# A decoder layer with routed experts: expert rows turned by VectorE, a shorter router, products of the identity in front

## The chip, the cores and the metric

One core of one Trainium2 chip runs the whole layer as one program. The metric is the device time of one execution in microseconds (us). The engines are TensorE (PE; its weight loads are PEld), VectorE (DVE), ScalarE (ACT), GpSimd (POOL) and the queue that issues the transfers, SyncE (SP). Each runs its own instructions in order; semaphores tie them together.

## The reference, cut to what matters

The layer is self-attention, cross-attention and a mixture of experts, each followed by a residual sum and a layer norm, on 8 x 112 = 896 rows of 512 numbers, in float32.

```
x = layernorm(x + attention(x))                 # 16 heads of 32, banded mask
x = layernorm(x + cross_attention(x, context))  # 16 heads of 128, 375 context rows, q and k normalised
scores = sigmoid(x @ gate_w.T)                  # 8 experts
topk   = top_k(scores + gate_bias, 2)           # two experts for each row
w      = scores[topk] / sum(scores[topk])
out    = silu(g) * y @ shared_dw.T              # shared part, hidden width 704
for e in experts: out += (silu(g_e) * u_e) @ down_w[e].T * w_e   # hidden width 352
x = layernorm(x + out)
```

## The kernel before, in words

Nearly every product of two float32 matrices is made of three one-pass products of a high and a low part (`three_products`, lines 86 to 88): ACT rounds a block to its high part, DVE or POOL subtracts to get the low part, PE multiplies. A few small or less exact ones are plain float32 products, which the profile records twice for each product.

**Start.** SP loads two blocks of weights, then the turned input `xT` in four pieces, one for each 128 rows of features, then `wv`. ACT makes `xT_hi` half a piece at a time, DVE `xT_lo`. PE waits for the first `xT_lo` and begins the 48 products of the first projections. The identity `ident` and the mask are set by POOL; a semaphore `consts_set` counts to 8 when both are there.

**Cross-attention.** Slots of one pair of heads and one batch element each, in a hardware loop. Its last slots are written out by hand, so that the last output products (`output(t, bank)`, t = 2 to 6), the residual sums, the layer norm and the turning of the result (`turn(pe, t)`) run into each other. In that order stand `output(4, y_ps)`, then a wait for the sum that reads `y_ps` (`added(4)`), then `join` (the last 12 value products, into the same bank, `o_view`), `turn` 2 and 3, `output` 5 and 6, `turn` 4, the first shared up-product `dense_up(0)`, `turn` 5 and 6, and then the router.

**Router.** `logits_T` makes the eight logits of all rows (24 products of 448 columns), ACT copies them, `logits` turns them back in seven small products, ACT takes the exponential, DVE chooses two experts for each row (`choose`, result `picked`). `places` counts on PE, with `before` (a strict triangle of ones) and `every` (all ones), how many earlier rows chose the same expert: one product, six that carry the earlier tiles on, and seven that make the total. DVE makes from it the owner of each block and the slot of each row (`place`). POOL then scatters the 896 rows twice to `sorted_x` in DRAM, SP fetches weights by owner.

**Shared part and blocks.** The shared hidden width is done in two units of 352, A ahead of the blocks and B behind them: `dense_up(k)`, then `dense_down(unit, t)` for t = 0 to 6. Between them lie NB = 21 blocks of 128 sorted rows. For block j, PE does:

```
block_up(j)        # 24 products of 352 columns: 4 pieces of x by 2 halves by 3
turn_block(j + 1)  # 4 float32 transposes of the next block's rows into PSUM
block_down(j - 1)  # 3 plain float32 products of 512 columns
turn_hidden(j)     # 3 transposes of the hidden rows
```

`turn_block(0)` stands ahead of `dense_down(0, 6)`. ACT does for each block: silu, `block_x(j + 1)` (the high part of the turned rows, read from PSUM), the copy of the turned hidden rows, and `up_high(j + 2)`, four casts that round the up-weights of the block after next. DVE does: two of the four low parts of these weights (`up_low`), the product of the hidden halves, `block_low(j + 1)` (the low part of the rows, one input in PSUM, one in SBUF), and the copy of an output block (`take`). POOL does the other two low parts.

SP's order for block j is: `load_up(j + 4)` once `block_up(j)` is done, `load_x(j + 3)`, `load_down(j + 3)`, `store_y(j - 1)`. The weights have a ring of three buffers. A block moves 1408 KB of up-weights, 768 KB of down-weights, 256 KB of rows in and 256 KB out. After the last block, unit B's `dense_up` needs the up-weights of load 22 (`LAST_U`), which go the same way as a block's.

## Time and profile before

| | |
|---|---|
| median of three runs | 1074.83 us (1074.69 to 1076.5) |
| the profiled execution | 1065.3 us |
| its span, first to last instruction | 1063.6 us |
| PE / PEld / DVE / ACT / POOL busy | 96% / 85% / 66% / 49% / 50% |
| granted TensorE clock, mean | 0.999 |
| share of PE in the chain that ended last | 74% |

The profiled execution is 1.7 us longer than its span, and 9.5 us shorter than the median of the three runs. The cross-attention loop ends at about 785 us, the router lies between 812 and 830 us, the blocks between 860 and 1010 us, unit B behind them.

### The profile page before, as it was taken

What the parts mean: (1) busy time and instruction counts of PE and PEld (TensorE: products, weight loads), DVE (VectorE), ACT (ScalarE), POOL (GpSimd) and SP (SyncE); (2) the same over time, 40 slices, a digit from 0 to 9 for tenths busy, and PEclk for the clock granted to TensorE, in tenths of its full rate; (3) what the DMA queues carried; (4) which work ended last, traced back from release to release, by engine and by line L of the source; (5) the groups of instructions that cost most, each with busy time, mean ns of one, the idle gap of its engine ahead of it and who ended that gap; (6) DMA issues with size and microseconds to landing.
All of it is one profiled execution on the core that took longest, in us unless ns stands there. A gap on an engine that the chain in (4) does not pass through costs nothing.

```text
span 1063.6 us, 20152 instructions
## 1 busy us (share of the span) xinstructions
PE 1021.0 (96%) x7006; PEld 906.5 (85%) x7006; DVE 703.5 (66%) x1452; ACT 523.7 (49%) x1033; POOL 530.0 (50%) x515
## 2 busy tenths in 40 slices
PE   6999888999999999999999999999998999999997
PEld 5866667899999999999999999999886887887786
DVE  4277776777777777777777777767785454554457
ACT  5355545555545555555555455455542345655520
POOL 0156766864633633643643643643572645444543
PEclk9999999999999999999999999999999999999999
DMA  8100104324333233233233233224220769999843
GB/s 285 69 31 2 60 16 136 149 113 147 121 112 116 95 110 115 95 110 115 94 110 115 96 108 115 98 107 152 91 73 1 299 243 376 389 390 378 309 120 108
DMA packets 44697, 153.46 MB, mean 144 GB/s; under 512 B 3704, under 2 KB 3704, under 8 KB 41568
## 3 DMA queue, kind: packets, MB, share of 16 engines
q1 hardware_dynamic: 42400, 145.38, 38.0%
q0 software_dynamic: 2240, 7.34, 2.1%
q8 instruction: 34, 0.56, 0.2%
q14 instruction: 23, 0.19, 0.0%
HBM read 130.04 MB, written 22.66 MB: 144 GB/s over the span
## 4 chain that ended last, share of the span: by engine, by line
PE 74%; DVE 4%; POOL 3%; issue 2%; ACT 2%; POOLq 0%; DVEq 0%; ACTq 0%
PE xa_y_ps L86 6%; PE xa_y_ps L88 6%; PE xa_y_ps L87 5%; PE ex_raw_ey_ps L2078 5%; PE ex_raw_gu_ps L86 4%; PE ex_raw_gu_ps L88 4%; PE ex_raw_gu_ps L87 4%; PE xa_c_ps L1871 4%; PE xa_c_ps L1867 4%; PE xa_c_ps L1866 4%; PE xa_turn_ps L1948 3%; PE xa_turn_ps L1904 3%; PE front_k_ps L86 3%; PE front_k_ps L88 3%; PE front_k_ps L87 3%
## 5 line engine op out<-in xcount | busy, mean ns | idle before, releaser
L1218 POOL TENSOR_TENSOR xa_probs<-xa_probs,xa_inv_sum 112x750 f32<-112x750 f32 x63 | 97.8, 1552 | 75.8 <-DVE xa_inv_sum L1545 75.8
L1494 DVE TENSOR_TENSOR xa_kT_lo<-xa_turn_ps,xa_kT_hi 128x750 fp32r<-128x750 f32 x63 | 59.2, 940 | 99.8 <-ACT xa_kT_hi L1306 99.7
L1203 POOL TENSOR_TENSOR k_ms<-k_ss,sum_eps 125x6 f32<-125x6 f32 x63 | 12.5, 198 | 210.9 <-DVE k_ss L1510 210.9
L1866 PE MATMUL xa_c_ps<-xa_probsT_hi,xa_nat 125*128 125x224 f32 x384 | 92.3, 274 | 2.7 <-ACT xa_probsT_hi L1322 2.7
L1867 PE MATMUL xa_c_ps<-xa_probsT_hi,xa_nat 125*128 125x224 f32 x384 | 92.3, 275 | 0.0
L1206 POOL TENSOR_TENSOR k_inv<-k_ms,neg_half 125x6 f32<-125x6 f32 x63 | 83.4, 1324 | 8.3 <-POOL k_ms L1203 6.6
L1322 ACT CAST xa_probsT_hi<-xa_turn_ps 125x672 fp32r<-125x672 f32 x62 | 44.6, 719 | 87.1 <-PE xa_turn_ps L1948 87.1
L1328 ACT ACTIVATE xa_probs<-xa_scores_ps,xa_bias,xa_q_scale 112x375 f32<-112x375 f32 x126 | 82.6, 662 | 5.7 <-DVE xa_bias L1520 4.4
L1866 PEld LDWEIGHTS xa_c_ps<-xa_probsT_hi,xa_nat 125*128 125x128 f32 x384 | 73.6, 192 | 3.5 <-issue 3.1
L1867 PEld LDWEIGHTS xa_c_ps<-xa_probsT_hi,xa_nat 125*128 125x128 f32 x384 | 73.5, 191 | 0.5
L86 PE MATMUL front_k_ps<-land_xa_wk_hi,land_xa_ctx 128*125 128x256 f32 x252 | 71.4, 283 | 1.4 <-DVE front_k_hat L1537 1.0
L87 PE MATMUL front_k_ps<-land_xa_wk_hi,land_xa_ctx 128*125 128x256 f32 x252 | 70.9, 281 | 0.0
L88 PE MATMUL front_k_ps<-land_xa_wk_lo,land_xa_ctx 128*125 128x256 f32 x252 | 70.8, 281 | 0.0
L1302 ACT ACTIVATE front_k_sq<-front_k_ps 125x512 f32<-125x512 f32 x63 | 37.7, 598 | 61.5 <-PE front_k_ps L88 60.2
L1871 PE MATMUL xa_c_ps<-xa_probsT_lo,xa_nat 125*128 125x224 f32 x384 | 64.0, 275 | 0.7 <-DVE xa_probsT_lo L1526 0.7
L1510 DVE TENSOR_REDUCE k_ss<-front_k_sq 125x6 f32<-125x768 f32 x63 | 59.7, 948 | 5.6 <-ACT front_k_sq L1310 5.6
L416 POOL TENSOR_TENSOR sa_masked<-sa_masked,sa_row_max 112x448 f32<-112x448 f32 x32 | 30.2, 945 | 66.1 <-DVE sa_row_max L647 65.4
L1489 DVE TENSOR_TENSOR xa_cT_lo<-xa_c_ps,xa_cT_hi 128x448 fp32r<-128x448 f32 x61 | 38.0, 623 | 37.9 <-ACT xa_cT_hi L1297 37.9
L1310 ACT ACTIVATE front_k_sq<-xa_k_ps 125x256 f32<-125x256 f32 x63 | 24.2, 385 | 70.8 <-PE xa_k_ps L88 70.8
L1516 DVE TENSOR_REDUCE xa_row_max<-xa_scores_ps 112x2 f32<-112x750 f32 x63 | 58.5, 928 | 0.0
L1297 ACT CAST xa_cT_hi<-xa_c_ps 128x448 fp32r<-128x448 f32 x61 | 32.5, 533 | 52.7 <-PE xa_c_ps L1871 52.7
L1526 DVE TENSOR_TENSOR xa_probsT_lo<-xa_turn_ps,xa_probsT_hi 125x672 fp32r<-125x672 f32 x62 | 53.1, 857 | 5.3 <-ACT xa_probsT_hi L1322 4.7
(371 smaller groups left out, 3486.4 us busy)
## 6 DMA issues: line engine op xcount, KB each, us to landing
xa_nat<-ctx_split SPq DMA_DIRECT2D x56, 750.0 KB
ex_raw_raw<-in_w_units SPq DMA_DIRECT2D x15, 1408.0 KB, 7.7
ex_raw_raw<-in_w_units SPq DMA_DIRECT2D x15, 768.0 KB, 7.7
land_ex_raw<-in_w_units SPq DMA_DIRECT2D x8, 1408.0 KB, 7.7
land_ex_raw<-in_w_units SPq DMA_DIRECT2D x8, 768.0 KB, 7.7
ctx_split<-xa_nat SPq DMA_DIRECT2D x8, 750.0 KB
sorted_x<-ex_raw_y_sb SPq DMA_DIRECT2D x7, 768.0 KB, 10.5
ex_raw_x_nat<-sorted_x SPq DMA_DIRECT2D x21, 256.0 KB, 8.1
```

The lines of the kernel that those rows point to most:

```text
L86: pe.matmul(out, st_hi, mv_hi, start=first, stop=False)
L87: pe.matmul(out, st_lo, mv_hi, start=False, stop=False)
L88: return pe.matmul(out, st_hi, mv_lo, start=False, stop=last)
L1206: pool.tensor_tensor(k_inv[0:KT, :], k_ms[0:KT, :], env["neg_half"][0:KT, 0:2 * KT_N], ALU.pow).then_inc(sem["kinv_done"], 1)
L1218: pool.tensor_tensor(probs[0:T, u % 2], probs[0:T, u % 2], inv_sum[0:T, u % 2, :].unsqueeze(2).broadcast_to([T, 2, KV]), ALU.mult).then_in ...
L1328: act.activation(probs[0:T, u % 2, h, :], scores_ps[0:T, h, 0:KV], ACT.Exp, bias=bias[0:T, u % 2, h:h + 1], scale=q_scale[0:T, u % B // HA ...
L1494: dve.tensor_tensor(kT_lo[:, :, 0:KV], turn_ps[:, :, 0:KV], kT_hi[:, :, 0:KV].bitcast(F32), ALU.subtract).then_inc(sem["kT_lo_done"], 1)
L1510: dve.tensor_reduce(k_ss[0:KT, :], k_sq[0:KT, :].rearrange("p (a d) -> p a d", d=XA_DH), AX_X, ALU.add).then_inc(sem["kss_done"], 1)
L1516: dve.tensor_reduce(row_max[0:T, u % 2, :], scores_ps[0:T, :, 0:KV], AX_X, ALU.max).then_inc(sem["max_done"], 1)
L1866: pe.matmul(c_view[:, c], nat[0:KT, u % 2, 0, at], probsT_hi[0:KT, :, cols], start=(t == 0), stop=False)
L1867: pe.matmul(c_view[:, c], nat[0:KT, u % 2, 1, at], probsT_hi[0:KT, :, cols], start=False, stop=False)
L1871: mm = pe.matmul(c_view[:, c], nat[0:KT, u % 2, 0, at], probsT_lo[0:KT, :, cols], start=False, stop=(t == KT_N - 1))
```

## The change

It has eight parts.

1. The input `xT` is loaded in eight pieces instead of four, each with a semaphore of its own, and ACT waits for each half.
2. PE waits for `consts_set` 8 and makes sixteen float32 products of the identity with itself before it waits for the first weights.
3. The last `join` writes to a bank of `turn_ps` (`o_last`) and stands ahead of the wait `added(4)`, which moves behind `turn` 2 and 3.
4. `turn` 5 and 6 stand inside `dense_up(0)`, behind 18 of its 24 products.
5. The gate's high and low part lie side by side (`gate_hl`), so that one product makes both: 16 products instead of 24. The seven turns are 16 wide, begin when the first half is copied, and DVE adds the two parts (`logits_added`) ahead of the exponential.
6. `before`, `every` and `picked` become one-pass operands; the seven products of the total become one, and DVE sums its result.
7. `turn_block` leaves PE. The rows of a block are fetched by four transfers, each into 32 partitions in runs of 128 numbers (512 bytes), and DVE turns them in squares of 32 into `x_raw` in SBUF, in one instruction; `block_x` and `block_low` read `x_raw`. The experts' up-weights are reordered on the host to suit. `turn_block(j + 1)` stands first in DVE's work for block j.
8. `turn_block(0)` and `block_low(0)` follow DVE's sum of tile 5, and `dense_down(0, 6)` moves behind `block_up(0)`.

```diff
             for c in range(DC):
-                sp.dma_start(xT_raw[:, c, :], xT[:, c, :]).then_inc(sem[f"xT_{c}_loaded"], 16)
+                for g in range(2):
+                    cols = slice(g * HT, (g + 1) * HT)
+                    sp.dma_start(xT_raw[:, c, cols], xT[:, c, cols]).then_inc(sem[f"xT_{c}_{g}_loaded"], 16)
...
+            wait(pe, "consts_set", 8)
+            for _ in range(16):
+                pe.matmul(y_ps[:, 0:P], ident[:], ident[:], start=True, stop=True)
             wait(pe, "wq_lo_done", 1)
...
+        o_last = turn_ps[:, 0, 0:4 * T].rearrange("p (h t) -> p h t", h=2)
...
             def load_x(j):
                 if j >= 2:
                     sp.wait_ge(xs["xb_turned"], j - 1)
-                sp.dma_start(x_nat[:, j % 2, :], sorted_x[j * P:(j + 1) * P, :]).then_inc(xs[f"x_{j % 2}_loaded"], 16)
+                rows = sorted_x[j * P:(j + 1) * P, :].rearrange("(b t) d -> t b d", t=SQUARE)
+                for a in range(P // SQUARE):
+                    part = x_nat[a * SQUARE:(a + 1) * SQUARE, j % 2, :].rearrange("t (b d) -> t b d", d=P)
+                    sp.dma_start(part, rows[:, :, a * P:(a + 1) * P]).then_inc(xs[f"x_{j % 2}_loaded"], 16)
...
-                act.copy(xb_hi[:], et_ps[:, 0, :]).then_inc(xs["xb_hi_done"], 1)
+                act.copy(xb_hi[:], x_raw[:]).then_inc(xs["xb_hi_done"], 1)
...
+            def turn_block(j):
+                dve.wait_ge(xs[f"x_{j % 2}_loaded"], 64 * (j // 2 + 1))
+                if j >= 1:
+                    dve.wait_ge(xs["xb_lo_done"], j)
+                dve.transpose(x_raw[:].rearrange("p (c b t) -> p b c t", c=DC, t=SQUARE), x_nat[:, j % 2, :].rearrange(
+                    "p (b c t) -> p b c t", c=DC, t=SQUARE)).then_inc(xs["xb_turned"], 1)
...
-                dve.tensor_tensor(xb_lo[:], et_ps[:, 0, :], xb_hi[:].bitcast(F32), ALU.subtract).then_inc(xs["xb_lo_done"], 1)
+                dve.tensor_tensor(xb_lo[:], x_raw[:], xb_hi[:].bitcast(F32), ALU.subtract).then_inc(xs["xb_lo_done"], 1)
...
+                dve.wait_ge(xs["logits_ready"], 1)
+                pair = et_ps[:, 0, 0:2 * TILES * E].rearrange("p (t a e) -> p t e a", a=2, e=E)
+                dve.tensor_reduce(score[:], pair, AX_X, ALU.add).then_inc(xs["logits_added"], 1)
                 dve.wait_ge(xs["logits_exp"], 1)
...
-            block_low(0)
-            add_shared(TILES - 1, 0)
+                if t == TILES - 2:
+                    turn_block(0)
+                    block_low(0)
             for j in range(NB):
                 n = UPS + j
+                if j + 1 < NB:
+                    turn_block(j + 1)
                 up_low(j + 2)
...
-                        mm = three_products(pe, et_ps[0:E, g, 0:HT], gate_hi[:, c, :], gate_lo[:, c, :],
-                                            xT_hi[:, c, cols], xT_lo[:, c, cols], c == 0, c == DC - 1)
+                        pe.matmul(et_ps[0:2 * E, g, 0:HT], gate_hl[:, c].rearrange("p a e -> p (a e)"), xT_hi[:, c, cols],
+                                  start=(c == 0), stop=False)
+                        mm = pe.matmul(et_ps[0:E, g, 0:HT], gate_hi[:, c, :], xT_lo[:, c, cols], start=False, stop=(c == DC - 1))
...
-                for t in range(TILES):
-                    mm = pe.matmul(et_ps[:, 1, 0:E], every[:], picked[:, t, :], start=(t == 0), stop=(t == TILES - 1))
-                mm.then_inc(xs["places_ready"], 1)
-
-            def dense_up(k, base, w_hi, w_lo):
+                pe.matmul(et_ps[:, 1, 0:TILES * E], every[:], picked[:].rearrange("p t e -> p (t e)"), start=True,
+                          stop=True).then_inc(xs["places_ready"], 1)
+
+            def dense_up(k, base, w_hi, w_lo, between=None):
...
             output(4, y_ps)
-            added(4)
-            join(N + 2, 0, N // 2 - 1)
+            join(N, 0, N // 2 - 1, o_last)
             turn(pe, 2)
             turn(pe, 3)
+            added(4)
...
             for t in range(TILES - 1):
                 dense_down(0, t, 0)
-            turn_block(0)
-            dense_down(0, TILES - 1, 0)
             pe.wait_ge(xs["consts_set"], 2)
             for j in range(NB):
                 block_up(j)
-                if j + 1 < NB:
-                    turn_block(j + 1)
-                if j >= 1:
+                if j == 0:
+                    dense_down(0, TILES - 1, 0)
+                else:
                     block_down(j - 1)
                 turn_hidden(j)
```

## Rows read from the trace of the kernel before

**Rows 1.** The page: busy us (share) xinstructions of each engine.
```profile
PE 1021.0 (96%) x7006; PEld 906.5 (85%) x7006; DVE 703.5 (66%) x1452; ACT 523.7 (49%) x1033; POOL 530.0 (50%) x515
```

**Rows 2.** Timeline of the start: start us, duration us, engine, line, operation [idle before].
```profile
2.08 0.59 POOL L383 TENSOR_SCALAR_AFFINE_SELECT sa_mask<-sa_mask 112x448 f32<-112x448 f32 x1
9.06 0.71 PE L86 MATMUL sa_scores_ps<-xT_hi,sa_qk_hi 128*128 128x448 f32 x1 [9.06 <-DVE xT_lo L580]
12.94 0.37 PE L87 MATMUL sa_scores_ps<-xT_hi,sa_qk_lo 128*128 128x448 f32 x1
20.54 0.39 PE L86 MATMUL sa_proj_ps<-land_wv_wv_hi,xT_hi 128*112 128x512 f32 x1
```

**Rows 3.** Timeline, the end of cross-attention and the router, 797 to 823 us.
```profile
798.48 0.34 PE L86 MATMUL xa_y_ps<-xa_cT_hi,xa_wv_hi 128*128 128x224 f32 x1 [0.87 <-DVE resid L1718]
798.40 2.09 POOL L112 TENSOR_SCALAR resid<-resid,ln_mv,ln_rstd 128x512 f32<-128x512 f32 x1
812.17 0.37 PE L86 MATMUL ex_raw_et_ps<-xT_hi,ex_raw_gate_hi 128*8 128x448 f32 x1 [1.56 <-DVE xT_lo L138]
817.85 0.60 PE L1988 MATMUL ex_raw_et_ps<-ident,ex_raw_logitsT 8*128 8x8 f32 x7 [0.61 <-ACT ex_raw_logitsT L1429]
```

**Rows 4.** Timeline, the counts of `places`.
```profile
823.48 1.46 PE L1998 MATMUL ex_raw_et_ps<-ex_raw_picked,ex_raw_every 128*128 128x48 f32 x12
824.80 1.71 PE L2001 MATMUL ex_raw_et_ps<-ex_raw_picked,ex_raw_every 128*128 128x8 f32 x14
```

**Rows 5.** Timeline, from unit A to the second block, 859 to 868 us.
```profile
859.17 0.60 PE L2042 MATMUL ex_raw_et_ps<-ident,ex_raw_x_nat 128*128 128x128 f32 x4
859.37 0.69 DVE L1674 TENSOR_TENSOR resid<-resid,ex_raw_ey_ps 128x512 f32<-128x512 f32 x1 [0.58 <-PE ex_raw_ey_ps L88]
861.70 0.33 PE L86 MATMUL ex_raw_gu_ps<-land_ex_up_lo,ex_raw_xb_hi 128*128 128x352 f32 x1
862.51 3.20 DVE L1572 TENSOR_TENSOR ex_low_low<-ex_raw_raw,land_ex_up_hi 128x704 fp32r<-128x704 f32 x2
862.51 4.74 POOL L1243 TENSOR_TENSOR ex_low_low<-ex_raw_raw,land_ex_up_hi 128x704 fp32r<-128x704 f32 x2 [9.18 <-ACT land_ex_up_hi L1354]
865.55 0.60 PE L2042 MATMUL ex_raw_et_ps<-ident,ex_raw_x_nat 128*128 128x128 f32 x4
```

**Rows 6.** Timeline of one steady block, from the end of `block_up` at 943.14 us.
```profile
943.14 0.60 PE L2042 MATMUL ex_raw_et_ps<-ident,ex_raw_x_nat 128*128 128x128 f32 x4
943.58 2.74 PE L2078 MATMUL ex_raw_ey_ps<-ex_raw_raw,ex_raw_hT 128*128 128x512 f32 x6
946.40 0.41 PE L86 MATMUL ex_raw_gu_ps<-land_ex_up_lo,ex_raw_xb_hi 128*128 128x352 f32 x1
949.28 3.48 POOL L1243 TENSOR_TENSOR ex_low_low<-ex_raw_raw,land_ex_up_hi 128x704 fp32r<-128x704 f32 x2 [3.68 <-ACT land_ex_up_hi L1354]
```

**Rows 7.** Windows: stretch, length; PE PEld DVE ACT POOL busy; PEclk, DMA share, GB/s.
```profile
871.50:878.67 7.17, 7.17 (x39) 5.66 (x38) 3.60 (x5) 4.22 (x7) 3.03 (x3) 1.00 1.02 397
878.67:1000.46 121.79, 121.79 (x631) 96.26 (x630) 61.19 (x85) 71.78 (x119) 59.26 (x35) 1.00 1.00 383
```

**Rows 8.** Transfers 242.6 to 243.9 us: packets by size; then the queue.
```profile
DMA packets 101, 0.16 MB, mean 119 GB/s; under 512 B 51, under 2 KB 51, under 8 KB 101
q1 hardware_dynamic: 101, 0.16, 34.0%
```

**Rows 9.** Up-weight transfers, 864 to 900 us, then 972 to 1000: KB, us to landing.
```profile
ex_raw_raw<-in_w_units SPq DMA_DIRECT2D x4, 1408.0 KB, 7.1
...
ex_raw_raw<-in_w_units SPq DMA_DIRECT2D x3, 1408.0 KB, 9.1
```

**Rows 10.** Timeline, last up-weight load, its casts, and unit B's first product.
```profile
993.48 0.34 SPq L1100 DMA_DIRECT2D ex_raw_raw<-in_w_units  x1
1004.37 2.83 ACT L1354 CAST land_ex_up_hi<-ex_raw_raw 128x704 fp32r<-128x704 f32 x4
1010.44 0.45 PE L86 MATMUL ex_raw_gu_ps<-xT_hi,land_ex_up_hi 128*128 128x448 f32 x1
```

More of the change, by code:

```diff
@@ L53 @@
 HPAD = HC * P
+SQUARE = 32
 def hold(eng, sem, i, per, n):
@@ L468, in _ @@
             for c in range(DC):
-                wait(act, f"xT_{c}_loaded", 16)
                 for g in range(2):
                     cols = slice(g * HT, (g + 1) * HT)
+                    wait(act, f"xT_{c}_{g}_loaded", 16)
                     act.copy(xT_hi[:, c, cols], xT_raw[:, c, cols]).then_inc(sem["xT_hi_done"], 1)
@@ L740, in _ @@
             values(0, range(DC))
-            wait(pe, "consts_set", 8)
             def scores(u):
@@ L1174, in set_consts @@
                           allow_small_or_imprecise_dtypes=True).then_inc(xs["more_consts"], 1)
-                pool.memset(before, 1.0).then_inc(xs["more_consts"], 1)
-                pool.memset(every, 1.0).then_inc(xs["more_consts"], 1)
+                pool.memset(before.bitcast(F32), 1.0).then_inc(xs["more_consts"], 1)
+                pool.memset(every.bitcast(F32), 1.0).then_inc(xs["more_consts"], 1)
                 pool.memset(upto, 1.0).then_inc(xs["more_consts"], 1)
                 pool.wait_ge(xs["more_consts"], 6)
-                pool.affine_select(out=before, in_=before, compare_op=ALU.is_gt, fill=0.0, base=0,
+                pool.affine_select(out=before, in_=before.bitcast(F32), compare_op=ALU.is_gt, fill=0.0, base=0,
                                    pattern=[[1, P]], channel_multiplier=-1).then_inc(xs["more_consts"], 1)
@@ L1618, in place @@
                 dve.wait_ge(xs["places_ready"], 1)
-                step(dve.tensor_tensor(over[:], et_ps[:, 1, 0:E].unsqueeze(2).broadcast_to([P, E, TILES]), level[:], ALU.is_gt))
+                step(dve.tensor_reduce(n_tiles[:], et_ps[:, 1, 0:TILES * E].rearrange("p (t e) -> p e t", e=E), AX_X, ALU.add))
+                step(dve.tensor_tensor(over[:], n_tiles[:].unsqueeze(2).broadcast_to([P, E, TILES]), level[:], ALU.is_gt))
                 step(dve.tensor_reduce(n_tiles[:], over[:], AX_X, ALU.add))
@@ L1873, in context_of, with join @@
                 mm.then_inc(sem["c_ready"], 1)
-            def join(s, i, j):
+            def join(s, i, j, view):
                 hold(pe, sem["wv_lo_done"], i, 1, j // HALF + 1)
@@ L1957, in slot @@
                 if j is not None:
-                    join(s, i, j)
+                    join(s, i, j, o_view)
                 u = s - 2
@@ L2016, in dense_up @@
                                             xT_hi[:, d, cols], xT_lo[:, d, cols], d == 0, d == DC - 1)
+                        if between is not None and (half, d) == (1, 1):
+                            between()
                 mm.then_inc(xs["up_ready"], 1)
@@ L2034, in dense_down @@
                 mm.then_inc(xs["y_ready"], 1)
-            def turn_block(j):
-                pe.wait_ge(xs[f"x_{j % 2}_loaded"], 16 * (j // 2 + 1))
-                if j >= 1:
-                    pe.wait_ge(xs["xb_lo_done"], j)
-                for c in range(DC):
-                    mm = pe.transpose(et_ps[:, 0, c * P:(c + 1) * P], x_nat[:, j % 2, c * P:(c + 1) * P], ident[:])
-                mm.then_inc(xs["xb_turned"], 1)
             def block_up(j):
@@ L2125, in _ @@
             added(2)
-            join(N, 0, N // 2 - 2)
+            join(N, 0, N // 2 - 2, o_view)
             context_of(u - 1, 0)
@@ L2148, in _, with last_turns @@
             pe.wait_ge(xs["up_lo_g"], 2)
-            dense_up(0, 0, up_hi, up_lo)
-            turn(pe, 5)
-            turn(pe, 6)
+            def last_turns():
+                turn(pe, 5)
+                turn(pe, 6)
+            dense_up(0, 0, up_hi, up_lo, last_turns)
             pe.wait_ge(norm["turn_lo"], TILES)
@@ L2240, with quarters, unit @@
     shared_gw, shared_dw = a["L0_ffn_shared_gw"], a["L0_ffn_shared_dw"]
-    def unit(up, down):
+    def quarters(w):
+        return w.reshape(P // SQUARE, DC, SQUARE, w.shape[1]).transpose(0, 2, 1, 3)
+    def unit(up, down, rows=chunks):
         tail = np.zeros((HC * P - HID, D), down.dtype)
-        return np.concatenate([chunks(up).reshape(P, -1), chunks(np.concatenate([down, tail], axis=0)).reshape(P, -1)], axis=1)
-    units = [unit(a["L0_ffn_up_w"][e].T, a["L0_ffn_down_w"][e].T) for e in range(EXPERTS)]
+        return np.concatenate([rows(up).reshape(P, -1), chunks(np.concatenate([down, tail], axis=0)).reshape(P, -1)], axis=1)
+    units = [unit(a["L0_ffn_up_w"][e].T, a["L0_ffn_down_w"][e].T, quarters) for e in range(EXPERTS)]
     for s in range(SHARED // HID):
```

53 lines of the change are left out of this document (30 added, 23 removed).

## Prediction

> **What bounds it now.** I read the page first: PE is busy 96% of the span [rows 1], so a gain is PE time removed, or a wait of PE removed. Then the timeline, at the four places that the change touches. At the start PE has nothing until 9.06 us, and then 48 products take until 20.54 us [rows 2]. Until 12.94 us they start 0.37 us apart, behind it 0.20. The clock column says full for both, but the ratio is that of 1.2 to 2.4 GHz, so I count 3.88 us at half speed. Near the router PE stands for 0.87, 1.56 and 0.61 us [rows 3]. From unit A to the second block it is nearly without gaps [rows 5], and in the blocks it has none: PE is busy 121.79 of 121.79 us over 17 blocks, 7.164 us each [rows 7]. The view that decides is the last column but one of the same row: the transfer engines are 1.00 busy as well, at 383 GB/s. A block moves 2688 KB, 2.75 MB, which at 383 GB/s is 7.2 us. So the blocks have two bounds at the same place. The landing times agree: an up-weight load lands 7.1 us behind its issue early on and 9.1 at the end [rows 9]. The queue grows slowly. What PE loses there, the transfers may not give back.
>
> **The start (parts 1 and 2).** The mask is set at 2.67 us [rows 2], so the sixteen products start at about 2.75. The trace shows no such product. Four transposes of 128 columns take 0.44 us [rows 6], 0.11 each and one record each; a plain float32 product is recorded twice, so I take 0.22 at full and 0.44 at half speed. With 3.9 us at half speed, as in [rows 2], nine products fill them, and the other seven end at 8.2 us. The first projection starts there instead of 9.06, since half a piece of input is there sooner: 0.85. All 48 then run at 0.20: 9.6 us instead of 11.48, 1.9. Together 2.7 us. If all sixteen ran at half speed they would end at 9.8, and 1.1 were left. Nothing behind is bound by time of day: PE is what later slots wait for, so I carry the gain through.
>
> **The router (parts 3 to 6).** The 0.87 us in front of the last `join` goes, but `turn` 3 still needs POOL, whose step that starts at 798.40 ends at 800.49 [rows 3]; I take 0.4 of it (0 to 0.87). With `turn` 5 and 6 six products of 0.2 earlier, their rounding lies beside these, and 1.25 of the 1.56 us goes. Eight gate products fewer are 1.6 us. The first three turns of the logits no longer wait: 0.2. In `places` 14 records take 1.56 us, from 824.80 to their last result, 0.11 each, and 12 take 1.3 [rows 4]. Small as they are, they cost their weight load, so one-pass products cost 0.11 each: eight instead of 27 records, 2.1 us less. DVE's two extra sums (about 0.25 each) lie beside `dense_up(1)`, and on the way to the slots, which still gets 1.8 shorter. Sum on PE: 0.4 + 1.25 + 1.6 + 0.2 + 2.1 = 5.55 us. Start and router give 8.25 (6.5 to 8.7).
>
> **From unit A to the blocks (part 8).** Before, `turn_block(0)` ran at 859.17, and `dense_down(0, 6)` covered the two rounding steps; `block_up(0)` started at 861.70 and ended at 865.55 [rows 5]. Now the cover is gone: DVE's sum of tile 5 ends at 860.06, then come DVE's turn, ACT's high part, DVE's low part. The turn is not in the trace; the nearest rows are 128x512 steps of DVE at 0.69 us, the upper bound twice that. I take 0.65 + 0.6 + 0.7 + 0.2 for hand-offs: start 862.2, end 866.05. PE stands 3 us. On this clock of before, the blocks start 0.5 us late.
>
> **The blocks (part 7).** PE drops four transposes, 0.44 us [rows 6]: 6.73 us a block. DVE (3.6 us a block) and ACT (4.2) have room [rows 7]. Two things do not shrink.
>
> First POOL: `block_up` at 946.40, POOL's two low parts from 949.28 to 952.76, needed at 953.56 [rows 6]: 6.36 us into the block, less than 6.73. But `block_low` now has both inputs in SBUF, as `up_low` has, and where two such DVE steps met POOL's they took 3.20 us, and POOL 4.74 instead of 3.48 [rows 5, 6]. One step of 0.69 would lengthen POOL by about 0.6: 7.06 us a block. The Trainium skill (SBUF — State Buffer, Who interferes with whom) says that DVE's second pair of ports is POOL's, and held exclusively for an instruction; rows 5 and 6 agree in kind.
>
> Second, the transfers. Their time for a block before lies between 6.93 (2.75 MB at the 397 GB/s of the best block shown) and 7.17 us [rows 7]; I take 7.1, because the queue grew. The rows' load changes from 128 packets of 2 KB to 512 of 512 bytes, 384 more. The price of a packet itself: in 1.3 us near 243 us, 34.0% of 16 engines is 7.07 us of engine time for 101 packets, 51 of them small, 0.16 MB [rows 8]. The bytes at 383 GB/s, 24 a nanosecond for one engine, take 6.7 of it, or 6.5 with the megabytes rounded down to 0.155; 0.4 to 0.6 us for 51 packets is 8 to 12 ns each. 384 such packets over 16 engines are 0.2 to 0.3 us. I take 0.43: the upper end and 0.13 more, because four transfers complete instead of one and may hinder each other (rival b). That makes 7.53 us a block (7.13 to 7.8). That is above PE's and POOL's.
>
> The sum on the clock of before: the first load of the series is issued at 866.4 and lands 7.2 later, 873.6; the 18th behind it, that of unit B, lands 18 x 7.53 = 135.5 later, at 1009.1. Three of ACT's four casts (2.12 of 2.83), POOL's 3.48 + 0.6 and 0.5 for hand-offs and for the rows' arrival ahead of DVE's low parts put unit B at 1015.8 instead of 1010.44 [rows 10]: 5.3 us lost. Before, issued at 993.48 and landed 9.1 later, the same load was there 1.8 us ahead of its cast at 1004.37. That was all the slack there was.
>
> **Total.** -8.25 + 5.3 = -2.95 us. Against the profiled execution's 1065.3 that is 1062.3; the median lies 9.5 above it, so 1071.9.
>
> **Rivals.** (a) The transfers have more to give than 383 GB/s. For it: the best block ran at 397. Against it: share 1.00 for 120 us, and the growing queue. Then POOL sets 7.06 us or PE 6.73. Unit B starts 20 x 6.73 + 2.8 behind 866.05, at 1003.4, 7.0 early, or with 7.06 at 1010.0: -8.7 in all with POOL (1066), -15.3 with PE (1059.5).
>
> (b) Slower: the narrow transfers. Each of the four fills 32 partitions. A load of 256 KB is 0.7 us of the 7.1; if its engines get in each other's way and it takes twice that, the block is 7.1 + 0.7 + 0.2 = 8.0 us, unit B 8.5 us later still than forecast, and the total +5.5 us (1080). It decides from 7.70 us a block, where the 8.25 are used up. Against it: the engines drift apart, and other transfers lie between. The Trainium skill (SBUF — State Buffer, Door 1: The DMA port swizzle) states it as a rule: partitions 0 to 31 reach 8 of 16 ports, half the rate, and two transfers in a row don't make up for it. No row here shows it; by its rate the load would take twice as long.
>
> (c) The front gives less: the 3 us that PE stands before `block_up(0)` cost it the clock as at the start, where 3.88 us at half speed cost 1.9. Then -1 us (1073.8). For it: no wait as long lies in the rows before a product at full speed, the longest is 1.56.
>
> **How the numbers follow.** The forecast 0.46 (1066 to 1075, by 7.2 to 7.7 us a block), (a) 0.16, (b) 0.24, (c) 0.14. 0.2% is 2.15 us, about what a measurement tells from no change, so faster ends at 1072.7: all of (a) and two thirds of the forecast, with a little of (c), 0.5. Same (to 1077.0), 0.26, from the rest of the forecast, (c), and the mild end of (b). Slower 0.24. Range 1064.5 to 1078.5: it leaves out PE-bound blocks below, and the narrow transfers at full price above.
>
> **What would show it.** PE starts projecting near 8.2 us with all starts 0.2 apart; seven turns of logits end 5 us earlier relative to 797 us; `places` takes under 1 us; about 3 us of idle PE ahead of `block_up(0)`; in the blocks PE waits, by name for the low parts of the up-weights, that is for a landing, at 7.5 us a block, with the share of the transfers at 1.00 and GB/s near 365. Blocks of 6.7 or 7.06 without waits for weights would be (a), of 8 us (b). Wrong would be, most of all, the price of a 512-byte packet: each 0.1 us a block is 1.8 us of the total.

## The result, and the profile after

The changed kernel takes 1082.38 us in the median of 11 runs (1080.44 to 1086.91), the kernel before in the same comparison 1075.86 us (11 runs, 1073.18 to 1079.27): ratio 1.0062, interval 1.0047 to 1.0078. It is slower by 6.5 us where I had forecast 2.95 us faster, and it lies above the range. The profiled execution took 1085.06 us, with a span of 1083.3.

First the page, busy time by engine; it answers to [rows 1]:

```profile
PE 1023.2 (94%) x6926; PEld 902.7 (83%) x6926; DVE 755.1 (70%) x1475; ACT 524.4 (48%) x1033; POOL 544.3 (50%) x515
```

TensorE has 80 records fewer and is a little longer busy, over a longer span. The timeline at the start, answering to [rows 2]:

```profile
2.72 6.28 PE L738 MATMUL sa_y_ps<-ident 128*128 128x128 f32 x32 [2.72 <-POOL sa_mask L387]
8.76 0.45 PE L87 MATMUL sa_scores_ps<-xT_hi,sa_qk_hi 128*128 128x448 f32 x1
9.04 0.36 PE L88 MATMUL sa_scores_ps<-xT_hi,sa_qk_lo 128*128 128x448 f32 x1
...
19.13 0.40 PE L87 MATMUL sa_proj_ps<-land_wv_wv_hi,xT_hi 128*112 128x512 f32 x1
```

The first projection starts 0.3 us earlier, and its products start 0.20 us apart nearly from the first on, TensorE's full speed. Near the router, answering to [rows 3, 4]:

```profile
798.50 0.66 PE L130 MATMUL xa_scores_ps<-ident,resid 128*128 128x128 f32 x4 [1.17 <-POOL resid L113]
...
808.45 0.38 PE L2009 MATMUL ex_raw_et_ps<-xT_hi,ex_raw_gate_hl 128*16 128x448 f32 x1 [0.35 <-DVE xT_lo L139]
...
812.49 0.42 PE L2020 MATMUL ex_raw_et_ps<-ident,ex_raw_logitsT 16*128 16x16 f32 x4 [0.33 <-ACT ex_raw_logitsT L1441]
...
817.79 0.19 PE L2028 MATMUL ex_raw_et_ps<-ex_raw_picked,ex_raw_before 128*128 128x56 f32 x1
817.81 0.81 PE L2031 MATMUL ex_raw_et_ps<-ex_raw_picked,ex_raw_every 128*128 128x48 f32 x6
818.48 0.27 PE L2033 MATMUL ex_raw_et_ps<-ex_raw_picked,ex_raw_every 128*128 128x56 f32 x1
```

All of that is as planned. From unit A to the blocks, answering to [rows 5]:

```profile
846.18 0.50 PE L87 MATMUL ex_raw_ey_ps<-land_ex_down_hi,ex_raw_h_hi 128*128 128x512 f32 x1 [3.79 <-DVE resid L1698]
...
848.18 0.63 PE L88 MATMUL ex_raw_ey_ps<-land_ex_down_hi,ex_raw_h_lo 96*128 96x512 f32 x1
...
856.96 0.70 DVE L1592 STREAM_TRANSPOSE ex_raw_x_raw<-ex_raw_x_nat 128x512 f32<-128x512 f32 x1
...
859.25 0.40 PE L87 MATMUL ex_raw_gu_ps<-land_ex_up_lo,ex_raw_xb_hi 128*128 128x352 f32 x1 [2.94 <-issue]
```

The 2.94 us in front of `block_up(0)` were in my sum. The 3.79 us were not. Five products later, from 847.75 us on, the down-products start 0.43 us apart instead of 0.23 for 3 us: TensorE's lower clock (1.2 GHz), granted 0.50 in that stretch. One block in the steady part, answering to [rows 6]:

```profile
942.50 0.40 PE L87 MATMUL ex_raw_gu_ps<-land_ex_up_hi,ex_raw_xb_hi 128*128 128x352 f32 x1 [1.15 <-DVE ex_raw_xb_lo L1600]
...
943.61 2.82 ACT L1366 CAST land_ex_up_lo<-ex_raw_raw 128x704 fp32r<-128x704 f32 x4 [1.74 <-DMA ex_raw_raw<-in_w_units]
...
944.98 0.71 DVE L1592 STREAM_TRANSPOSE ex_raw_x_raw<-ex_raw_x_nat 128x512 f32<-128x512 f32 x1 [1.98 <-DMA ex_raw_x_nat<-sorted_x]
...
945.62 3.14 DVE L1584 TENSOR_TENSOR ex_low_low<-ex_raw_raw,land_ex_up_lo 128x704 fp32r<-128x704 f32 x2
...
949.11 1.73 DVE L1600 TENSOR_TENSOR ex_raw_xb_lo<-ex_raw_x_raw,ex_raw_xb_hi 128x512 fp32r<-128x512 f32 x1
...
950.94 0.40 PE L87 MATMUL ex_raw_gu_ps<-land_ex_up_lo,ex_raw_xb_hi 128*128 128x352 f32 x1 [1.15 <-DVE ex_raw_xb_lo L1600]
```

From 942.50 to 950.94 is 8.44 us a block instead of 7.16. TensorE names VectorE as what it waits for, and the instruction is `block_low`, the low part of the rows; I had forecast a wait for the low parts of the weights. Two steps back on that chain both ScalarE's casts and VectorE's turn stand waiting for a transfer, one for weights, the other for rows. The windows and the transfers of the page, answering to [rows 7, 9]:

```profile
920.00:980.00 60.00, 51.35 (x240) 37.54 (x239) 45.95 (x44) 30.62 (x51) 31.29 (x15) 1.00 1.05 333
```

```profile
ex_raw_raw<-in_w_units SPq DMA_DIRECT2D x15, 1408.0 KB, 13.1
...
ex_raw_x_nat<-sorted_x SPq DMA_DIRECT2D x84, 64.0 KB, 10.6
```

The transfer engines are fully busy and move 333 GB/s, not 383. An up-weight load lands 13.1 us behind its issue in the median of the 15, not 7 to 9.

**The two profiles can't be compared as they stand.** They are 19.7 us apart, the medians 6.5. A second profile of the kernel before (`e0_before` below) has a span of 1073.6 instead of 1063.6, and both differences lie outside the blocks: 6.4 us up to the first block, in unit A, and 3.6 behind the blocks. The blocks took 7.16 us in both.

### The profile page after: what moved, and what is told of

It reads as the page before. It is cut to its first block, busy times and chain, and to the rows that moved or that the text cites. A ratio compares the mean times of both kernels' runs of the same rounds, so it can differ in the third digit from the quotient of the medians.

```text
span 1083.3 us, 20081 instructions
## 1 busy us (share of the span) xinstructions
PE 1023.2 (94%) x6926; PEld 902.7 (83%) x6926; DVE 755.1 (70%) x1475; ACT 524.4 (48%) x1033; POOL 544.3 (50%) x515
## 4 chain that ended last, share of the span: by engine, by line
PE 63%; DMA 6%; DVE 5%; issue 4%; POOL 4%; ACT 1%; SPq 1%; another core or an unknown queue 1%; POOLq 0%; DVEq 0%; ACTq 0%
PE xa_y_ps L87 6%; PE xa_y_ps L89 5%; PE xa_y_ps L88 5%; DMA ex_raw_x_nat<-sorted_x 5%; PE xa_c_ps L1900 4%; PE xa_c_ps L1896 3%; PE xa_c_ps L1895 3%; PE xa_turn_ps L1977 3%; PE xa_turn_ps L1933 3%; PE ex_raw_gu_ps L87 3%; PE ex_raw_gu_ps L89 3%; PE ex_raw_gu_ps L88 3%; PE front_k_ps L87 3%; PE front_k_ps L89 3%; PE front_k_ps L88 3%
## 5 line engine op out<-in xcount | busy, mean ns | idle before, releaser
L1538 DVE TENSOR_TENSOR xa_probsT_lo<-xa_turn_ps,xa_probsT_hi 125x672 fp32r<-125x672 f32 x62 | 53.1, 857 | 5.2 <-ACT xa_probsT_hi L1334 4.7
## 6 DMA issues: line engine op xcount, KB each, us to landing
ex_raw_raw<-in_w_units SPq DMA_DIRECT2D x15, 1408.0 KB, 13.1
land_ex_raw<-in_w_units SPq DMA_DIRECT2D x8, 768.0 KB, 13.1
```

## The experiments

The ratio is to the kernel before, run on the same chip. "Late blocks" is the mean distance of the starts of `block_up` over the last 13 blocks of the profile, from the timeline. e0 to e3 ran on one chip, e4 to e7 on a second, e8 to e12 on a third, e13 to e15 on a fourth; the kernel before took 1075.3, 1076.7, 1065.9 and 1066.0 us on them. "4 x 32, 512 B" is four transfers into 32 partitions each, in packets of 512 bytes; a load is called narrow when its transfers fill fewer than 128 partitions, and wide otherwise. The edits are shown shortened. e4 to e7 leave rows or features in the wrong places and so don't compute the layer; they do the same work and are there to measure only.

| run | rows' load | turned by | ratio (interval) | late blocks, us |
|---|---|---|---|---|
| kernel before (e0) | 1 x 128 partitions, 2 KB | PE | 0.9998 (0.9979 to 1.0017) | 7.16 |
| changed kernel | 4 x 32, 512 B | DVE | 1.0062 (1.0047 to 1.0078) | 8.49 |
| e1_front | 1 x 128, 2 KB | PE | 0.9926 (0.9900 to 0.9952) | 7.16 |
| e2_wide4 | 4 x 128, 512 B, dealt | DVE | 1.0298 (1.0271 to 1.0325) | 9.49 |
| e3_blocks (old front) | 4 x 32, 512 B | DVE | 1.0154 (1.0120 to 1.0188) | 8.22 |
| e4_narrow2k | 4 x 32, 2 KB | DVE | 1.0009 (0.9986 to 1.0032) | 8.02 |
| e5_wide2k | 1 x 128, 2 KB | DVE | 0.9889 (0.9855 to 0.9923) | 6.88 |
| e6_wide512 | 4 x 128, 512 B | DVE | 0.9890 (0.9856 to 0.9924) | 6.88 |
| e7_narrow_pe | 4 x 32, 512 B | PE | 1.0058 (1.0039 to 1.0076) | 8.41 |
| e8_order | 4 x 32, 512 B, order 0 2 1 3 | DVE | 1.0053 (1.0038 to 1.0068) | 8.09 |
| e10_act_queue | 4 x 32, 512 B, ScalarE's queue | DVE | 0.9974 (0.9959 to 0.9988) | 7.61 |
| e11_scatter | 1 x 128, 2 KB | PE | 0.9922 (0.9905 to 0.9939) | 7.16 |
| e12_halves | 2 x 64, 2 KB | PE | 1.0022 (1.0007 to 1.0037) | 8.13 |
| e13_three | as e10, three buffers | DVE | 0.9976 (0.9962 to 0.9990) | 7.52 |
| e14_start (parts 1, 2) | 1 x 128, 2 KB | PE | 0.9981 (0.9965 to 0.9996) | 7.16 |
| e15_front_again | 1 x 128, 2 KB | PE | 0.9925 (0.9909 to 0.9941) | 7.16 |

**e0_before**: the kernel before, unchanged.

> The kernel before, unchanged, for a second profile of it. The profile on record took 1065.3 us where its other executions took 1073 to 1079, and the changed kernel's profile took 1085.1 where its median is 1082.4: the two profiles are 19.7 us apart, the medians 6.5. If the executions differ in one place, this profile shows it: I expect the difference behind 785 us, either in the scatter of the rows (end of unit A), or in blocks that take 7.3 to 7.6 us instead of 7.16 because their transfers are slower. If the blocks take 7.16 here too and the time is near 1075, the difference lies elsewhere. Ratio 1.00.

Ratio 0.9998. The extra time is behind 785 us and not in the blocks. In unit A, TensorE's timeline and then ScalarE's:

```profile
855.85 0.79 PE L86 MATMUL ex_raw_ey_ps<-land_ex_down_hi,ex_raw_h_hi 128*128 128x512 f32 x1 [5.98 <-DVE resid L1674]
```

```profile
851.11 0.54 ACT L1369 ACTIVATE ex_raw_silu_g<-ex_raw_gu_ps 96x448 f32<-96x448 f32 x1 [8.44 <-remote]
```

The sum of tile 0 stands in VectorE's order behind the work on ScalarE's last silu, and that silu is late. It starts when the weights' and the scatter's transfers drain (their share falls from 0.95 to 0.21 at 851.0 us). In the first profile the transfers drained as late, and the same silu ran at 846.03; so why it waits here is open. The last part is longer too: from unit B's first product to the end 56.8 us instead of 53.1. It goes with the chip and not with the change: e0 to e7 show 55 to 58 us there, e8 to e15, on chips where the kernel before takes 1066 us, 53.1. (Each chip had one group of runs, so chip and hour can't be told apart.)

**e1_front** takes back parts 7 and 8:

```diff
-                for a in range(P // SQUARE):
-                    ...                                        # the four narrow transfers
+                sp.dma_start(x_nat[:, j % 2, :], sorted_x[j * P:(j + 1) * P, :]).then_inc(...)
-            dve.transpose(x_raw...)                            # block_x, block_low read x_raw
+            for c in range(DC): pe.transpose(et_ps[:, 0, ...]) # block_x, block_low read et_ps
```

> The change without parts 7 and 8: the start and the router as changed, PE turns the rows again, one transfer for each block, and the hand-over from unit A as before. If the front is worth the 8.25 us of my sum, the time is 8 us below the kernel before (ratio 0.992 to 0.993). The profile of the changed kernel shows another thing: the shared down-products began 7.7 us earlier (838.1 instead of 845.8) but the last one ahead of the blocks ended only 3.0 earlier, since PE stood 3.8 us for the sum of tile 0, which waits for the scatter of that tile, and ran at half speed for 3 us behind it. By that theory this kernel gains only 2.5 to 4 us (ratio 0.996 to 0.998), with the same wait in its profile.

0.9926: 8 us faster, the first of the two answers. The 3.7 us of TensorE are in its profile as well (846.16, `[3.73 <-DVE resid L1687]`), but the kernel before has its own 5.98 on such a chip, so they don't eat the gain. My second answer had taken the shorter profile of the kernel before for the typical one.

**e2_wide4** deals the same pieces to the four transfers by rows instead of by partitions:

```diff
-                rows = sorted_x[j * P:(j + 1) * P, :].rearrange("(b t) d -> t b d", t=SQUARE)
-                for a in range(P // SQUARE):
-                    ...                                        # the four narrow transfers
+                rows = sorted_x[j * P:(j + 1) * P, :].rearrange("(b t) (a d) -> b a t d", t=SQUARE, d=P)
+                for b in range(P // SQUARE):
+                    sp.dma_start(x_nat[:, j % 2, b * P:(b + 1) * P], rows[b]).then_inc(...)
```

> The changed kernel with the same 512-byte pieces to the same places, but dealt to the four transfers the other way: each transfer brings 32 rows and writes 128 partitions by 512 bytes instead of 32 partitions by 2 KB in four runs. Narrow transfers (rival b): the blocks fall from 8.2 us to 7.3 to 7.6, and the time by 10 to 15 us, below the kernel before (ratio to it 0.993 to 0.998). Packet size: the blocks stay at 8.0 to 8.3 us and the time at a ratio of 1.005 to 1.008. VectorE's order (the turn waits for the rows ahead of the low parts of the weights, and these collide with GpSimd's): no change either.

1.0298, which none of the three answers expected. The transfers view of 955 to 961 us, in columns of 0.15 us, and the issue on SyncE of the load whose packets run from 957.4 us on:

```profile
DMA  9989989988998897413223222233234997953969
GB/s 539 403 375 451 526 375 526 451 375 375 451 451 375 375 526 300 167 48 137 65 68 137 65 65 65 79 85 85 79 82 119 160 324 164 160 119 119 198 205 317
```

```profile
951.44 5.18 SPq L1130 DMA_DIRECT2D ex_raw_x_nat<-sorted_x  x4
```

For some 2.5 us only 2 or 3 tenths of the engines work, and SyncE needs 5.2 us to issue four of them. Two things changed at once, so this run doesn't answer its question; e6 asks it again. The Trainium skill (DMA: Bandwidth & Descriptors, Why a DMA increments its semaphore by 16 and not by 1) says that a transfer runs on as many engines as the largest number up to 16 that divides the slowest dimension of both its patterns. The trace agrees: in the source pattern that dimension is 4, so it would be 4 engines of 16, and the row shows a share of 2 or 3 tenths.

**e3_blocks**: the kernel before with part 7 alone (the lines of the diff for `load_x`, `turn_block`, `block_x`, `block_low` and the order of the weights), `turn_block(0)` on VectorE ahead of `block_low(0)` and the old cover of `dense_down(0, 6)`.

> The kernel before with part 7 alone: rows in four narrow transfers, turned by VectorE; start, router and the hand-over with its cover as before. By my sum for the blocks at 7.53 us it would lose 5 us (ratio 1.005); by the 8.2 us a block that the changed kernel's profile shows, (8.2 - 7.16) x 20 = 21 us in terms of the fast profile, and, where the front's gain is only 3 us, 9 to 10 us in terms of the medians: ratio 1.008 to 1.012. If it loses under 5 us, the front is what fails.

1.0154 (16.6 us), above the range that I gave: the blocks fail, not the front. 0.9926 and 1.0154 together give 1.008; the change has 1.0062.

**e4_narrow2k, e5_wide2k, e6_wide512, e7_narrow_pe** part width, packet size and who turns:

```diff
 # e4: whole rows into 32 partitions, four times (b = 0 to 3)
+                    sp.dma_start(x_nat[b * SQUARE:(b + 1) * SQUARE, j % 2, :],
+                                 sorted_x[j * P + b * SQUARE:j * P + (b + 1) * SQUARE, :])
 # e5: one transfer
+                sp.dma_start(x_nat[:, j % 2, :], sorted_x[j * P:(j + 1) * P, :])
 # e6: a quarter of the columns into all partitions, four times
+                    sp.dma_start(x_nat[:, j % 2, cols], sorted_x[j * P:(j + 1) * P, cols])
 # e7: e1_front with the change's own load_x
```

> The changed kernel with its four transfers into 32 partitions each, but each brings 32 whole rows in packets of 2 KB (128 packets a block instead of 512). The rows stand in x_nat as before, so VectorE's squares mix features of different rows and the output is not the reference's; the work of every engine is the same. If narrowness costs (rival b), the blocks stay near 8.2 us and the time at a ratio of 1.004 to 1.008. If the 512-byte packets cost, the blocks fall to 7.2 to 7.5 us and the time to 0.992 to 0.997.

> The changed kernel with the rows' load of before: one transfer, 128 packets of 2 KB, x_nat in the order of the rows (the output is then not the reference's); VectorE turns as in the change. It shows the change without what it does to the transfers. My sum for GpSimd was 7.06 us a block, for TensorE 6.73: if the transfers are all that the change loses on, the blocks take 7.06 to 7.2 us and the time a ratio of 0.990 to 0.994. If VectorE's order is the cause (its turn waits for rows, then its two low parts collide with GpSimd's, and the low part of the rows comes last), the blocks stay above 7.5 us here too.

> The changed kernel with four transfers for a block that each bring one quarter of the columns of all 128 rows: 512 packets of 512 bytes as in the change, but each transfer writes 128 partitions (the quarters are not dealt out, so the output is not the reference's). With the run that has narrow transfers of 2 KB it parts the two: packets alone give 8.0 to 8.3 us a block and a ratio of 1.004 to 1.008, narrowness alone 7.2 to 7.5 us and 0.992 to 0.997. SyncE's issues should be near 0.35 to 0.5 us each; in the run with rows dealt by 32 they took 1.3 us each, which made SyncE the bound.

> The kernel with the changed front and the old blocks (e1_front), but rows fetched by the change's four narrow transfers of 512-byte packets; TensorE turns what it finds in x_nat, so the output is not the reference's. If the transfers alone set the 8.2 us, the blocks take 8.2 us here too (ratio 1.004 to 1.008). If the change's loss needs VectorE's turn as well, they stay at 7.16 to 7.5 us (0.992 to 0.998).

Windows of 920 to 980 us (busy PE, PEld, DVE, ACT, POOL; then clock, share of the transfer engines, GB/s), of e4, e5, e6 and e7 in this order:

```profile
920.00:980.00 60.00, 53.39 (x254) 40.50 (x253) 48.76 (x45) 33.24 (x55) 31.46 (x16) 1.00 1.03 353
```

```profile
920.00:980.00 60.00, 60.00 (x294) 46.83 (x293) 44.51 (x53) 36.69 (x62) 29.34 (x18) 1.00 1.01 401
```

```profile
920.00:980.00 60.00, 60.00 (x293) 46.56 (x292) 45.09 (x53) 36.57 (x61) 29.35 (x18) 1.00 1.03 402
```

```profile
920.00:980.00 60.00, 53.36 (x265) 40.53 (x264) 24.87 (x35) 28.95 (x49) 24.28 (x14) 1.00 1.05 332
```

With 512 packets of 512 bytes, e6 moves as many GB/s as e5 with 128 of 2 KB, and its ratio is the same. Wide packets of 512 bytes cost the blocks nothing here, and neither does it cost to have four transfers instead of one. Narrow transfers cost with either packet: 353 GB/s for 2 KB, 332 for 512 bytes. My answers for e4 had left this middle out: its 1.0009 lies between them. From wide to narrow the ratio rises by 0.012 with 2 KB packets (e5 to e4), and another 0.005 comes with the packets of 512 bytes (e4 to the changed kernel, or to e7 on the same chip). Both wide runs came out below what I had given. And e7, without VectorE's turn, has the changed kernel's 8.4 us, its 332 GB/s and its ratio. So VectorE's order isn't the cause: its waits in the timeline above are for a transfer, and when the rows come wide they are gone, with `block_low` as long as in the changed kernel:

```profile
939.61 1.72 DVE L1597 TENSOR_TENSOR ex_raw_xb_lo<-ex_raw_x_raw,ex_raw_xb_hi 128x512 fp32r<-128x512 f32 x1
```

That row is of e5, whose blocks take 6.88 us.

**e8_order, e12_halves, e10_act_queue, e13_three** ask what "narrow" is, and whether it can be hidden:

```diff
 # e8
-                for a in range(P // SQUARE):
+                for a in (0, 2, 1, 3):
 # e12: e1_front, rows by halves
+                for a in range(2):
+                    part = slice(a * P // 2, (a + 1) * P // 2)
+                    sp.dma_start(x_nat[part, j % 2, :], sorted_x[j * P + a * P // 2:j * P + (a + 1) * P // 2, :])
 # e10: out of SyncE's order, into ScalarE's, behind its four casts
                 up_high(j + 2)
+                if j + 3 < NB:
+                    act.wait_ge(xs["xb_turned"], j + 2)
+                    load_quarters(act, j + 3, range(P // SQUARE))
 # e13: e10 with x_nat [3, D], the load waits for xb_turned j + 1
```

> The changed kernel with its four narrow transfers in the order 0, 2, 1, 3 of their quarters of the partitions instead of 0, 1, 2, 3. Nothing else differs. If what costs is that one transfer's engines all write into half of the ports, neighbours on the other half should help where the engines have drifted apart: blocks of 7.5 to 8.0 us instead of 8.2 to 8.5, ratio 1.000 to 1.004. If two transfers in a row don't make up for it, as the skill has it, the blocks stay and the ratio is 1.004 to 1.008.

> The changed front with the old blocks, the rows fetched by two transfers of 64 rows into 64 partitions each, 2 KB packets, the output being the reference's. If only 32 partitions are too narrow, the blocks stay at 7.16 us and the ratio at 0.992. If a span of 64 partitions is as bad as one of 32, as the Trainium skill's port table says, they cost what the four transfers of whole rows into 32 partitions cost: 13 us between that run (1.0009) and the one with one wide transfer (0.989), or, since this kernel starts from 7.16 instead of 6.86 us a block, about 7 us: ratio 0.997 to 1.001.

> The changed kernel with the rows' four transfers (from block 3 on) issued from ScalarE's queue, behind its four casts of the next weights, so that the 16 engines take the narrow packets in turns with the wide ones of the weights on SyncE's queue. If the loss is that for the length of the narrow transfers all engines crowd the same ports, mixing them with wide packets gives most of it back: blocks of 6.9 to 7.4 us and a ratio of 0.988 to 0.996, the output being the reference's. If the narrow packets cost the same engine time wherever they stand, the blocks stay above 8 us. ScalarE pays 4 issues of 0.4 to 0.7 us a block, of which it has 1.7 free ahead of silu; the rest could put up to 1 us on the path of the hidden rows.

> As the run with the rows' transfers on ScalarE's queue, but with three buffers of rows instead of two, so that a load may be issued one block earlier (it waits for the turn of block j instead of j + 1). In that run seven of the turns waited 1.1 to 4.4 us for their rows although the engines' share was no higher than 1.02, and the blocks took 6.7 to 9.3 us; the other blocks took 6.7 to 7.0. If the late rows are what was left, all blocks take 6.8 to 7.2 us here and the ratio is 0.986 to 0.992. If mixing gives back only half of what the narrow transfers cost, the blocks stay at 7.5 us on average and the ratio at 0.996 to 0.998, with the engines' share at 1.00 or more and waits for weights.

The order changes little: 1.0053, and the late blocks at 8.09 us are still 1.2 above the wide ones. Halves of 64 partitions are as bad as quarters of 32: TensorE turns here, and its 7.16 us become 8.13; the ratio of 1.0022 lies just above the 0.997 to 1.001 that I gave for this answer. Issued by ScalarE instead of SyncE the narrow transfers cost about half, between my two answers. Windows of e10:

```profile
920.00:980.00 60.00, 55.36 (x263) 42.08 (x264) 42.56 (x49) 34.18 (x58) 28.31 (x16) 1.00 1.02 362
```

362 GB/s, and a ratio of 0.9974: better than both kernels of the case, worse than the front alone. The third buffer gave nothing more (0.9976), though nine turns still waited for rows, 18.0 us in all; why they did, with a load issued two blocks ahead, is open.

**e11_scatter**: e1_front, with the second block's weights issued behind the scatter.

```diff
             load_up(1, units[0]); load_down(1, units[0])
-            load_up(2, units[1]); load_down(2, units[1])
             for t in range(TILES): sp.wait_ge(xs[f"scattered_{t}"], 32)
             load_x(0)
+            load_up(2, units[1]); load_down(2, units[1])
```

> The changed front with the old blocks, and the weights of the second block (2.2 MB) issued behind the scatter of the rows instead of ahead of it. In the profiles of the front alone TensorE stood 3.7 us for the sum of tile 0, which waits for that tile's scatter, and then ran 3 us at half speed. If the scatter is late because the weights' transfers share the engines with it (share 1.00 for 15 us), it ends some 5 us earlier, the wait goes, and the time falls by 3 to 5 us against the front alone: ratio 0.988 to 0.990. If the wait is GpSimd's own pace (14 issues of 1.27 us), nothing changes, 0.992 to 0.993. If the second block's weights come too late, TensorE waits for them before its second block and the gain is less.

0.9922, as the front alone. It ran on a chip that doesn't have the wait (0.61 us where e0 to e7 stood 3.7 to 6.7), so its question stays open.

**e14_start, e15_front_again** part the front's gain:

```diff
 # e14: the kernel before and
+                for g in range(2): ...           # xT in eight pieces
+            for _ in range(16): pe.matmul(y_ps[:, 0:P], ident[:], ident[:], start=True, stop=True)
 # e15: e1_front unchanged
```

> The kernel before with parts 1 and 2 alone (input in eight pieces, sixteen products of the identity in front). My sum for them was 2.7 us with a lower bound of 1.1: ratio 0.9975 (0.997 to 0.999). The front as a whole took 0.9926 at its first run, so parts 3 to 6 would be the other 0.995. If the start gives nothing that lasts, the ratio is 1.000 and the router is worth all 8 us.

> The changed front with the old blocks once more, to stand beside the two others on the same chip: 0.9926 as before (0.990 to 0.995) if its gain doesn't hang on the chip. The kernel before took 1075 us on two of the chips and 1066 on another; in the profiles of the slower ones TensorE stood 3.7 to 6.7 us for the scatter of tile 0, on the faster one 0.6. If the front's earlier scatter gains or loses by that wait, the ratio moves by up to 0.3% from chip to chip.

0.9981 for the start, 2.0 us (0.4 to 3.7), and 0.9925 for the whole front, so 0.9944, 6 us, for the router. A second kind of chip gives the front the same ratio as the first.

## Why the prediction was wrong

**The step that failed** is the price of the rows' load: "I take 0.43 ... That makes 7.53 us a block". The late blocks of the changed kernel take 8.49, by rival (b)'s mechanism and near its price: it gave 8.0 us a block and 1080 us, and the result is 1082.4. I had sized a packet, 0.2 to 0.3 us for 384 small ones, and added 0.13 for narrowness. The term for narrowness, 0.13 us, is what was too small. A wide load fits in 6.88 us with all else, whatever its packets (e5, e6), so the narrow one costs at least 8.02 - 6.88 = 1.1 us a block with 2 KB, and 8.49 - 6.88 = 1.6 with 512 bytes. The reason that I held against (b) was that the engines drift apart and other transfers lie between. With the quarters in another order (e8) most of the cost stayed; with other transfers between them (e10) half of it went.

Narrowness is more than a transfer at half rate: a load of 256 KB is 0.7 us wide, so its doubling would be 0.7, not 1.1 to 1.6. The packet records in the traces show where the rest is. Each is the mean duration of the packets that start between 920 and 980 us, times their number in a block, over 16 engines. As the engines are never idle there, the parts, with 0.7 to 0.9 for the stores, add up to about the block.

| us a block | rows | down-weights, packets of 6 KB | up-weights, 11 KB |
|---|---|---|---|
| kernel before | 0.72 | 2.08 | 3.62 |
| e5, wide, 2 KB | 0.71 | 1.94 | 3.53 |
| e6, wide, 512 B | 0.87 | 2.05 | 3.41 |
| e4, narrow, 2 KB | 0.84 | 2.61 | 3.65 |
| changed kernel, narrow, 512 B | 1.33 | 2.81 | 3.74 |
| e10, narrow, ScalarE's queue | 0.96 | 2.15 | 3.89 |

In the changed kernel the rows cost 0.6 us more than before, near the doubling that (b) named. But the down-weights, which are wide and stand right behind the rows in SyncE's order, cost 0.7 us more without having been touched, and neither my sum nor (b) had priced that. Why they slow down isn't shown. The small packets themselves cost 0.16 us wide (0.87 against 0.71), somewhat less than my 0.2 to 0.3. (Where the rows have packets of 2 KB, the stores have too, and both are taken at their common mean.)

The Trainium skill has the rule for the ports: 64 partitions reach no more of them than 32 (SBUF — State Buffer, Door 1: The DMA port swizzle), and two transfers can't be fused to reach all (Can I just issue two DMAs to hit both halves?). e12 agrees (8.13 us against 8.02), e8 nearly so; the ports themselves are seen in no run.

**The transfers as a bound.** That the blocks before had two bounds in one place was wrong by 4%: e5 and e6 move 401 and 402 GB/s at nearly the same share where [rows 7] have 383, so my 7.1 us for what is not narrow was 0.2 too much. Rival (a) was right in this. A share of 1.00 with 383 GB/s said that packets were always there, not that no more could pass; the queue of [rows 9] grew to 9 us, and the wide blocks would still have gone to 6.88.

**GpSimd.** I had its two low parts at 3.48 + 0.6 and so 7.06 us a block. In e5 they are still 3.48 us; it is VectorE's `block_low` that takes up to 1.77 us (1.72 in the row above) instead of 0.69, and with 6.88 us there is room for it. The clash was seen rightly and put on the wrong engine.

**The front** (forecast -8.25 us) measured -8.0 (0.9925 x 1066 us, the same ratio on two kinds of chip). The start: 2.0 us by ratio, where I had 2.7. By the timeline the 48 products are done at 18.44 us instead of 20.54, 2.1 us earlier. Further on the profiles scatter more: the product that waits 1.25 us for `sa_row_max` starts at 142.09 to 143.61 us in the fourteen with the changed start, at 144.50, 145.12 and 146.01 in the three without (e0, before, e3). The identity products fill the time to 8.76 instead of 8.2; the half-speed time goes as forecast. The router: in the profiles 5.70 us earlier to the first down-product of unit A (838.06, 695.01 us behind the product just named at 143.05; before 845.83, 700.71 behind 145.12), forecast 5.55. Its items hold: 0.35 us left of 1.56, 0.33 of 0.61, `places` 0.96 us (forecast under 1). `turn` 3 waited 1.17 us for GpSimd, which is why I had taken 0.4 of 0.87. (My 27 records for `places` should have been 28: 2, 12 and 14.)

**Unit A to the blocks.** 2.94 us of idle TensorE (forecast 3), the turn 0.70 us (0.65). Against e1_front, whose unit A runs alike up to 846.2 us, `block_up(1)` starts 0.9 us later (865.47 against 858.68 + 5.90 = 864.58); I had 0.5.

**Rival (c)**, that this wait costs the clock, is real, but not in every execution. In the profile of the change `block_up(0)` runs at 0.16 us a product from its second product on, and `block_up(1)` starts 6.22 us behind it; so in e5 and e10 (6.28, 6.22). In e2, e4 and e6 it is 7.82 us, in e8 7.57, in e13 9.08. There the same 2.94 us stand in front, and then, from somewhere between the first product and the seventh, products start 0.29 us apart at a granted clock of 0.50 for 2.5 to 6 us. In e6:

```profile
858.53 0.40 PE L87 MATMUL ex_raw_gu_ps<-land_ex_up_lo,ex_raw_xb_hi 128*128 128x352 f32 x1 [2.94 <-issue]
...
860.26 0.49 PE L89 MATMUL ex_raw_gu_ps<-ex_low_low,ex_raw_xb_hi 128*128 128x352 f32 x1
...
861.43 0.49 PE L87 MATMUL ex_raw_gu_ps<-land_ex_up_lo,ex_raw_xb_hi 128*128 128x352 f32 x1
```

Five of the eight profiles with part 8 pay 1.4 to 2.9 us; I had given (c) 1.9 us and 14%. The length of the wait alone doesn't decide it: behind the same 2.94 us the clock stayed at 1.00 in the other three. In the changed kernel's own profile it wasn't paid.

**The sum with the measured terms**: front -8.0, blocks about +14.5 (what is left to the result of +6.5; e7 against e1 gives +14.2 and part 7 alone measured +16.6), where I had -8.25 and +5.3. With the wide load of e5, parts 7 and 8 may be worth some 4 us more than the front alone (0.9889 against 0.9926, on two chips and with intervals that touch). But with such a load VectorE's squares of 32 don't make up a turned block, so this is no version of the layer.

## What to carry to other kernels

Price a load by the partitions that it reaches before its packet size: cutting one transfer of 128 partitions into two of 64 or four of 32 cost a saturated queue 1.0 to 1.6 us a block, cutting it into 512-byte packets over all 128 cost the blocks nothing. Ask also what stands behind such a load in the queue: half of the price here was paid by the next one. Where a work-saving step needs a narrow load, count it against the bytes in the same queue and not against the engine that is freed; of TensorE's 0.44 us a block, 0.28 were had, and only with the wide load. And compare two profiles only after profiling the kernel before once more on the chip of the second: here 10 of the 19.7 us between them are there without any change. The best version that computes the layer is the front alone, 0.9925 (0.9922 with the later weights of e11, no difference).

## What the runs showed of the hardware that I had not expected

- 64 partitions are no better than 32: late blocks 8.13 us (e12, TensorE turns) and 8.02 (e4), wide 7.16 and 6.88.
- Wide packets slow down behind a narrow load: the 6 KB packets of the down-weights took 0.35 us in the changed kernel, 0.33 in e4 and 0.34 in e12, against 0.24 to 0.27 where the rows come wide. The rows' own packets of 512 bytes took 0.042 us instead of 0.027 (e6).
- A transfer whose slowest source dimension is 4 kept 2 to 3 tenths of the engines busy at about 65 to 85 GB/s, and took SyncE 1.2 us in the mean to issue instead of 0.5 (e2, 920 to 1000 us).
- Narrow transfers issued by ScalarE, beside SyncE's wide ones, cost about half (362 GB/s against 333; late blocks 7.61 us against 8.49, wide 6.88).
- VectorE's step with both inputs in SBUF took 1.72 us beside GpSimd's instead of 0.69, while GpSimd's two stayed at 3.48 (e5).
- TensorE fell to its lower clock (1.2 GHz, granted 0.50) behind waits of 3.8 and 6.0 us, products of 512 columns 0.43 us apart for about 3 us; behind the same 2.94 us in five of eight profiles; in e2, e4, e7, e8 and e10 at 142.5 or 145.5 us, at once or 2 us behind a wait of 1.25 us; and at 1011 us in the changed kernel, behind blocks with gaps of 1 us each (products of 352 columns 0.29 instead of 0.16 apart).
- The kernel before took 1075 to 1077 us on two chips and 1066 on two others, and two profiles of it differ by 10 us, in unit A and behind the blocks; in the longer one ScalarE's last silu of unit A waited 8.44 us and started when the transfers had drained, in the shorter one it didn't wait for that.
